# A routed head taken first, film products and sums placed elsewhere, and feed-forward weights loaded ahead, in a decoder's cross-attention layer

## Reference, cut to what matters

```python
scores = einsum(Q, K) / sqrt(DH)              # 4 heads, 1024 tokens, 6404 context rows
topv, topi = jax.lax.top_k(scores, 32)        # per head and token
attn = zeros.at[topi].set(softmax(topv))
c_t = einsum(attn.mean(heads), x_vision @ Wv) * text_mask
x = layernorm(x_text)
scale_in, shift_in = split(c_t @ W_film_in + b_film_in)
x = x * (1 + gate * scale_in) + gate * shift_in
y = s4d(x)                                    # a long convolution, through a Fourier transform
scale_out, shift_out = split(c_t @ W_film_out + b_film_out)
y = y * (1 + gate * scale_out) + gate * shift_out
xt = x_text + y
h = gelu(layernorm(xt) @ W1 + b1) @ W2 + b2
return layernorm(xt + h)
```

## Time and profile before

| | us |
|---|---|
| median of three runs | 1678.64 |
| lowest and highest run | 1675.96, 1678.83 |
| the profiled execution | 1676.14 |
| its span in the trace | 1674.4 |
| searching and weighing, from the trace's first mask to its last | 669.7 to 1237.9 |
| film, transform and feed-forward | 1237.9 to 1320 |

### The profile page before, as it was taken

One profiled execution on the slowest core, in us unless ns is written; L12 is line 12 of the kernel. 1 busy time (PEld: TensorE's weight loads), 2 busy tenths in 40 slices (PEclk: granted clock), 3 DMA queues, 4 the chain that ended last, 5 costly groups with the idle time before them and its releaser, 6 DMA issues. The chain is left out here.

```text
span 1674.4 us, 19830 instructions
## 1 busy us (share of the span) xinstructions
PE 1375.7 (82%) x6709; PEld 738.1 (44%) x6763; DVE 1272.4 (76%) x2835; ACT 900.2 (54%) x1423; POOL 679.4 (41%) x463
## 2 busy tenths in 40 slices
PE   5677799999997758888898888989775449999798
PEld 2222344333334524455555555555555323333465
DVE  5999577856606679999999999999889556766433
ACT  4666211466633321777777777877852246666321
POOL 2665211122102042778787878878752120000012
PEclk9799899999997878999999999999897759999899
DMA  6000111000007741000000000000030300000000
GB/s 151 1 1 0 34 57 43 0 1 1 0 0 153 143 123 41 1 1 1 1 1 1 1 1 1 1 1 1 6 134 18 88 1 1 1 1 1 1 1 14
DMA packets 32482, 42.99 MB, mean 26 GB/s; under 512 B 14286, under 2 KB 25644, under 8 KB 30992
## 3 DMA queue, kind: packets, MB, share of 16 engines
q1 hardware_dynamic: 29820, 29.61, 6.1%
q10 hardware_dynamic: 2552, 12.02, 3.5%
HBM read 33.48 MB, written 8.14 MB: 25 GB/s over the span
## 5 line engine op out<-in xcount | busy, mean ns | idle before, releaser
L1628 PE MATMUL psum<-film_ka,film_context_qa 97*128 97x427 bf16 (+3 forms) x896 | 333.2, 372 | 83.2 <-DVE film_stage_e L1848 43.0
L2023 ACT ACTIVATE film_stage_e<-psum,film_stage_bias 128x512 f32<-128x512 f32 (+1 forms) x416 | 270.3, 667 | 104.8 <-PE psum L1630 96.8
L1806 DVE MAX8 film_stage_kept<-psum 128x8 f32<-128x213 f32 (+1 forms) x960 | 317.6, 373 | 8.5 <-PE psum L1630 8.2
L1630 PE MATMUL psum<-film_kb,film_context_qb 128*128 128x427 bf16 (+2 forms) x843 | 310.0, 368 | 0.0
L1848 DVE SCALAR_TENSOR_TENSOR film_stage_e<-psum,film_context_top,film_stage_e 128x512 f32<-128x512 f32 (+1 forms) x325 | 230.8, 716 | 10.8 <-ACT film_stage_e L2023 7.9
L1878 POOL TENSOR_TENSOR film_stage_e<-film_stage_e 128x1024 f32<-128x1024 f32 (+1 forms) x91 | 206.9, 2274 | 7.1
L1628 PEld LDWEIGHTS psum<-film_ka,film_context_qa 97*128 97x128 bf16 x896 | 93.0, 104 | 198.2 <-DVE film_stage_kept L1806 78.5
L1868 POOL TENSOR_TENSOR film_stage_e<-film_stage_e,film_stage_keep 128x512 f32<-128x512 f32 (+1 forms) x91 | 102.2, 1123 | 120.1 <-ACT film_stage_keep L1999 118.0
L1909 PEld LDWEIGHTS psum<-ctx_rows,film_stage_mean_T 128*128 128x128 f32 (+1 forms) x816 | 125.9, 198 | 31.7 <-issue 5.5
L3228 POOL TENSOR_TENSOR residual<-residual,top_expert_kept 128x1024 f32<-128x1024 f32 x7 | 16.4, 2350 | 295.0 <-DVE top_expert_kept L3185 295.0
L2991 DVE TENSOR_REDUCE gqa_attend_low<-psum 128x1 f32<-128x128 f32 (+7 forms) x128 | 94.1, 755 | 43.2 <-PE psum L2910 40.7
(11 more groups left out here) (546 smaller groups left out, 2554.1 us busy)
## 6 DMA issues: line engine op xcount, KB each, us to landing
film_kb<-film_k_rows ACTq DMA_DIRECT2D x4, 1601.0 KB
film_ka<-film_k_rows ACTq DMA_DIRECT2D x3, 1601.0 KB
ctx_T<-in_ctx_T SPq DMA_DIRECT2D x1, 2401.5 KB
gqa_experts_w<-in_L_ffn_W SPq DMA_DIRECT2D x1, 2048.0 KB
film_stage_e<-in_dft_ahead SPq DMA_DIRECT2D x1, 1728.0 KB, 7.7
film_k_rows<-cross_attention_film_hi SPq DMA_DIRECT2D x6, 256.0 KB, 2.1
film_k_rows<-cross_attention_film_mid SPq DMA_DIRECT2D x6, 256.0 KB, 2.1
film_k_rows<-cross_attention_film_low SPq DMA_DIRECT2D x6, 256.0 KB, 2.0
```

What stands on the lines that cost most here:

```text
L1628: pe.matmul(out, a["qa"][0:ROWS, h, rows], a["ka"][0:ROWS, h, c + b:c + b + cols], start=True, stop=False)
L1630: last = pe.matmul(out, a["qb"][:, h, rows], a["kb"][:, h, c + b:c + b + cols], start=False, stop=True)
L1806: last = dve.max(kept[:, h % 2, PER_PIECE * u + s, :], bank[:, lo:hi])
L2023: act.activation(e[:, n % RING, sub, 0:PIECES[u][1]], ps[:, SEARCH_BANKS + q % WEIGH_BANKS, 0:PIECES[u][1]], ACT.Exp, bias=bias[:, i % 2, ...
```

## The change

1. The routed head is head 0 and no longer head 3. ACT's mask of it and Pool's product come three slots earlier; Pool then waits for DVE's mask of head 3, and adds.
2. The film values of tiles 0 to 5 are made one in each of the last six weighing steps; tile 6 and tile 7 follow the loop.
3. The bias rows are made on Pool, in three instructions behind its own branch, and DVE waits for `bias_ready`.
4. PE makes the output's film products right behind its branch, ahead of `u`'s forward transform, into banks 4 to 7. ACT copies them then. The odd slots of the forward transform wait for the first copy, and the transform back for the second.
5. Pool prepares `rows_out` and `moved` as soon as its row is loaded, and its four sums wait for `u_odd`.
6. SP loads `rows_out` first, and `w_vo` behind `u`. The eight feed-forward loads are issued behind the transform's tables, into the end of `kb`, and the stage ends only when they have landed. The waits of the feed-forward block for them are gone.
7. In the feed-forward block ACT runs a GELU of one column right behind the square root.

```diff
     def masked_on_vector(n, h):
         if n >= (NT - 1) * NCH:
             return True
-        return h < 3
+        return h > 0
...
+        def film_values(i):
+            if i == 0:
+                pe.wait_ge(f["w_film_loaded"], 16)
+            pe.wait_ge(cc_ready, i + 1)
+            last = pe.matmul(ps[:, i // 2, (i % 2) * 2 * D:(i % 2 + 1) * 2 * D], c_ctx[:, i * P:(i + 1) * P],
+                             f["w_vf"][0:DC, :], start=True, stop=True)
+            if i % 4 == 3:
+                last.then_inc(film_done, 1)
...
+                if sub == 3 and n - FILM_FROM in range(NT - 2):      # FILM_FROM = STEPS - NT + 2
+                    film_values(n - FILM_FROM)
+
+        film_values(NT - 2)
+        pe.wait_ge(tok_ready, NT)
+        pe.transpose(ps[0:DC, 6, 3 * P:4 * P], c_tok[:], g["ident"][:]).then_inc(cc_psum, 1)
+        film_values(NT - 1)
...
-            limit = below[:, i % 2, h - 2:h - 1]
-            if n == NCH * i + (h == 2):
+            limit = below[:, i % 2, 0:1]
+            if n == NCH * i:
...
-    OUT_BANK = 2
+    OUT_BANK = 4
...
+            sp.dma_start(rows_out, ...).then_inc(rows_loaded, 16)
             sp.dma_start(u, ...).then_inc(u_loaded, 16)
+            sp.dma_start(w_vo[0:DC, :], a["w_vf_store"][:, 2 * D:]).then_inc(out_loaded, 16)
...
+            for name, src in (("w1", ...), ("b1", ...), ("g_ffn", ...), ("b_ffn", ...), ("w2", ...), ("b2", ...), ("gain", ...), ("shift", ...)):
+                sp.dma_start(a["ffn"][name], src).then_inc(a["ffn_loaded"], 16)
+            sp.wait_ge(a["ffn_loaded"], 16 * 8)
...
         @block.tensor
+            pe.wait_ge(out_loaded, 16)
+            for i in range(NT):
+                last = pe.matmul(flat[:, OUT_BANK * HALF + i * 2 * D:OUT_BANK * HALF + (i + 1) * 2 * D],
+                                 g["c_T"][0:DC, i * P:(i + 1) * P], w_vo[0:DC, :], start=True, stop=True)
+                if i % 4 == 3:
+                    last.then_inc(out_done, 1)
             pe.wait_ge(ahead_even, 16)
...
                 if slot == N_EVEN:
                     pe.wait_ge(u_odd, 1)
+                    pe.wait_ge(out_copied, 1)
...
+            pe.wait_ge(out_copied, 2)
             pe.wait_ge(y_even, 1)
...
-            pe.wait_ge(out_loaded, 32)
-            pe.wait_ge(z_ready, 1)
-            for i in range(NT):
...
         @block.gpsimd
-            pool.wait_ge(out_loaded, 32)
             pool.wait_ge(f["gate_loaded"], 16)
+            pool.wait_ge(f["bias_loaded"], 32)
+            pool.tensor_tensor(bias[1][:], bias[1][:], gate.to_broadcast([P, D]), ALU.mult)
+            link(pool.tensor_tensor(bias[0], bias[0], gate.to_broadcast([P, D]), ALU.mult))
+            link(pool.tensor_scalar(bias[0], bias[0], 1.0, None, ALU.add))
+            pool.sem_inc(bias_ready, 1)
+            pool.wait_ge(rows_loaded, 16)
             link(pool.tensor_tensor(rows_out, rows_out, gate.unsqueeze(1).to_broadcast([P, 2, D]), ALU.mult))
             link(pool.tensor_tensor(moved, g["xn"][:], tiles(rows_out[:, 1, :]), ALU.add))
             link(pool.tensor_scalar(rows_out[:, 0, :], rows_out[:, 0, :], 1.0, None, ALU.add))
+            pool.wait_ge(u_odd, 1)
...
         @block.vector
-            dve.wait_ge(f["bias_loaded"], 32)
-            dve.wait_ge(f["gate_loaded"], 16)
-            dve.wait_ge(first["mean_ready"], first["all_means"])
-            dve.tensor_scalar(bias[0][:], bias[0][:], gate[:, 0:1], 1.0, ALU.mult, ALU.add)
-            link(dve.tensor_scalar(bias[1][:], bias[1][:], gate[:, 0:1], None, ALU.mult))
+            dve.wait_ge(bias_ready, 1)
...
         @block.scalar                                  # of film_out_ffn
             root(act, norm[0]["rstd"], 1, var_ready[0], root_ready[0])
-            act.wait_ge(loaded, 16 * N_LOADS)
+            act.activation(warm[:], b_ffn, ACT.Gelu)
```

76 lines of the change are left out of this document (29 added, 47 removed).

## The result

| | before | after |
|---|---|---|
| runs, median (lowest to highest) | 1677.4 us (1675.96 to 1678.83) | 1659.67 us (1659.14 to 1659.78) |
| profiled execution, and its span | 1676.14, 1674.4 us | 1659.78, 1657.9 us |
| PE, DVE, ACT, Pool busy | as given under *Time and profile before* | 1369.8, 1255.7, 897.2, 678.3 us |

The ratio is 0.9894, 95% interval 0.9877 to 0.9911: faster by 1.1%. I forecast 1664.0 us, between 1654 and 1674.

The account below looks back on a forecast made before the run. DVE was taken to set the pace in searching and weighing, blocked by Pool's sums at tile boundaries. Part 1 -13.1, part 2 +0.4 and the rest -0.8 gave -13.5 us: 1662.6 or 1665.1, so 1664.0 us, between 1654 and 1674.

Parts of the forecast that it names:

- Part 1, the boundary: Six tile boundaries: M ends head 3's mask; DVE's small instructions end M+3.9, M+4.65; 1.65 us for 3.27, together -9.6.
- Part 1, the half clock: Behind six tile boundaries: a shorter stop may spare PE's clock fall, half of DVE's 0.53 us wait each, -1.5 us.
- Part 1, the last boundary: Seventh boundary, search over, DVE also waits 1.39 us for ACT: -2.0 us (0 to -3.5).
- Part 2, film values: Last six weighing steps: 0.45 us more PE work each nearly fits in PE's idle time, +0.4 us (0 to +2.7).
- Part 3, bias rows: Behind the branch: DVE gets its rows only after Pool's return and three instructions, +2.5 us (-0.5 to +4.9).
- Part 5, preparation, and part 4: Pool's addition moves from blocking the transform over j to the film, -0.3 us; output's products ahead hide, +0.2 us.
- Part 5, sums: Pool's four sums leave `inverse_odd`, -4.0 us, and block the fifth and sixth spectrum products, +1.3 us.
- Part 6: Loads and GELU table in the feed-forward block: ACT's wait for loads goes, -0.5 us for both (0 to -2.3).
- The rival of the moved boundaries: Tile boundaries: Pool's pair sum still falls on DVE's small instruction L1839, nothing won, about 1677 us; 8%.
- that of the bound Pool: Every step of seven tiles: Pool becomes the bound and steps lose time, at 0.25 us each about 1686 us; 5%.
- that of the late Pool: Behind the branch: Pool away 8.2 us and the transform at half clock, +4.9+2 for +2.7, about 1668 us; 7%.
- free boundaries: Tile boundaries: Pool's sums miss DVE's small instructions altogether and the half clock goes, -23 us, about 1655 us; 15%.

Follow-up runs that it names:

- e1: The kernel before with head 0 routed and nothing else changed; 1660.55 us, ratio 0.9897 against the kernel before.
- e10: e7 with all film values back behind the weighing, as in the kernel before; 1660.4 us, ratio 0.9897 against the kernel before.
- e4: The changed kernel with the bias rows made on DVE as before; 1659.45 us, ratio 0.9892 against the kernel before.
- e7: The changed kernel with Pool's three bias instructions ahead of its branch instead of behind it; 1655.39 us, ratio 0.9875 against the kernel before.
- e5: The changed kernel with DVE's three small instructions of each tile boundary moved to Pool; 1660.61 us, ratio 0.9897 against the kernel before.
- e11: The changed kernel without the one-column GELU that loads ACT's table early; 1660.19 us, ratio 0.99 against the kernel before.
- e6: The kernel before with DVE's three small instructions of each tile boundary moved to Pool; 1677.32 us, ratio 1.0002 against the kernel before.
- e8: e4 plus ten unread products on PE between the forward transform and the transform back; 1658.89 us, ratio 0.9889 against the kernel before.
- e9: e7 with Pool's second pair of sums behind DVE's first group of spectrum products; 1655.34 us, ratio 0.9876 against the kernel before.

## Why the prediction was right, and where it was off

- **Part 1, the boundary: right in size.** M+3.9 and M+4.65 were worked out; measured 1.73 us for a forecast of 1.65, and 1.56 a tile for 1.6. The reason was off, though: I had the third instruction meet Pool's product, but L1845 is free (162 ns) and the *second*, L1844, is blocked (604 ns), an operation with one input. And 0.58 of the 1.73 are still a wait for the logarithm.
- **Part 1, the half clock: undersized.** I charged 1.5 us for six boundaries, half of a small wait (0.53 each). The kernel before has five such falls at 0.82 us each, 4.1 in all; e1 wins them whole, and the changed kernel, with one fall left that costs 0.57, wins 3.5. In all the weighing won 15.1 us (15.5 in e1), forecast 12.7 (13.1).
- **Part 1, the last boundary: right in size by luck.** 2.2 for 2.0, but I had put it on the small instructions, which won nothing there (4.03 us for 4.05).
- **Part 2, film values: small, as forecast** (about +0.25 for +0.4), and "nothing, except that PE reaches its branch sooner" left out what mattered: once the film starts early, that exception is worth 1.2 us ahead of *ffn* and 2.3 with it (e10).
- **Part 3, bias rows: right.** +2.5 forecast, +2.33 measured, with Pool away 5.83 us. I had weighed a rule of the Trainium skill (Runtime: NRT & Kernel Launch, Instruction fetch mechanics): a taken branch out of the fetched window waits for a fetch. The trace agrees in that Pool pays as DVE does, 5.83 us on Pool and 5.65 on DVE in e4; that the time goes into a fetch no run shows. That the whole term could be had back by placing the three instructions ahead of the branch I didn't see.
- **Part 5, preparation, and part 4: right together, by two misses.** *Film* +1.24 and *over j* -1.58 make -0.34, forecast -0.3 and +0.2. But *over j* has the wait of 1.01 for a PE at half clock in it: without it (8.30 in e4 and e7) the preparation gives about -1.4, and part 4 costs about +1.1. I had the addition block the film for 2.3 us, and it blocked it for 1.24.
- **Part 5, sums: right.** -4.15 for -4.0, and +0.89 for +1.3: one product was blocked, not two.
- **Part 6: not decided.** -0.56 for -0.5, but *ffn* goes from 19.42 (e7) to 20.88 us (e5) among kernels with the same code there, so the match may be luck. ACT's wait of 2.32 us for the loads is gone (its first scaling now waits 0.44 for PE's transposes), and the GELU's table gives nothing (e11).

The sum was -13.5, and the profiled executions differ by 16.4: 2.4 of the missing 2.9 are the weighing, and 2.0 of these the clock. The step that failed is the size of the clock's term in part 1: -1.5 forecast, -3.5 measured. The rival of the moved boundaries fell with the medians of L1843 and L1845, that of the bound Pool with its 56.8 us of waiting, that of the late Pool with 5.83 us. Of "free boundaries" half came true: the clock now falls at two boundaries and no longer at six, but the sum still meets the small instructions.

## What to carry to other kernels

An instruction that is blocked for a microsecond on the busiest engine need not be worth that microsecond; ask what waits for its *result*, and whether that chain has something else as long in it. Here moving the instructions away from DVE (e5, e6) was worth nothing, and moving Pool's sums off them, with the clock that then stayed up, was worth 1%. By the timeline the chain's next limit is ACT with its two table loads. When several engines each leave for a long branch, what stands just ahead of it is free of the branch's time and what stands just behind pays all of it: put short work that others wait for in front (e7), and let the engine leave early (e10). And after each gain in a single-file stretch look at PE's clock in the next one: it can take a microsecond back (e8, e9). Compare two kernels' traces at the same place, and at more than one: here the fall of the clock is gone at four boundaries and still there at two.
